# A fused attention and feed-forward kernel: each projection dealt into its attention step in two runs instead of three

## The reference

```python
xn = _layernorm(x, axis=-1)                      # x: (4, 512, 512) float32
# attention: 16 heads of 32
q, k, v = (proj(Wq, bq), proj(Wk, bk), proj(Wv, bv))
scores = einsum('bhqd,bhkd->bhqk', q, k) / sqrt(32) + alibi_bias     # causal mask
ctx = einsum('bhqk,bhkd->bhqd', softmax(scores), v)
attn = ctx @ Wo + bo
# feed-forward 512 -> 2048 -> 512, its weights rebuilt from spline control points
ffn = einsum('bsi,hi->bsh', silu(gate) * up, down_w)
return x + attn + ffn
```

## Time and profile before

| | |
|---|---|
| median of 3 runs | 837.47 us (837.46 to 837.83) |
| the profiled execution | 838.84 us |
| its span, first to last instruction | 837.0 us |
| mean granted clock of TensorE | 0.922 of full |
| busy: PE, weight loads, DVE, ACT, POOL | 711.5, 563.2, 507.2, 439.3, 332.3 us |

### The profile page before, as it was taken

One profiled execution on the slowest core, in us unless ns is written; L12 is line 12 of the kernel. 1 busy time (PEld: TensorE's weight loads), 2 busy tenths in 40 slices (PEclk: granted clock), 3 DMA queues, 4 the chain that ended last, 5 costly groups with the idle time before them and its releaser, 6 DMA issues. The chain is left out here.

```text
span 837.0 us, 14001 instructions
## 1 busy us (share of the span) xinstructions
PE 711.5 (85%) x4884; PEld 563.2 (67%) x4884; DVE 507.2 (61%) x1289; ACT 439.3 (52%) x961; POOL 332.3 (40%) x191
## 2 busy tenths in 40 slices
PE   5678779889789888898898676677978999999997
PEld 4556557667677776676676565455766888888886
DVE  6286687798979888967888688556432222222212
ACT  4266576687657766756877672334332333233321
POOL 2343453444534545534544450112214325425434
PEclk9878789899979999898999799679898999999999
DMA  7982654553584346465437945756616646433201
GB/s 254 188 219 37 111 74 155 76 76 65 114 182 101 48 76 114 93 173 77 67 68 210 252 143 170 245 153 187 208 51 196 224 118 202 153 108 105 101 1 50
DMA packets 53023, 109.78 MB, mean 131 GB/s; under 512 B 6361, under 2 KB 6617, under 8 KB 51417
## 3 DMA queue, kind: packets, MB, share of 16 engines
q1 hardware_dynamic: 51368, 106.46, 51.2%
q10 hardware_dynamic: 1584, 2.43, 1.2%
HBM read 59.32 MB, written 25.17 MB: 101 GB/s over the span
## 5 line engine op out<-in xcount | busy, mean ns | idle before, releaser
L1132 POOL TENSOR_TENSOR work<-work 128x1280 f16<-128x1280 f32 x64 | 168.4, 2632 | 235.2 <-DVE work L816 234.9
L1029 ACT ACTIVATE work<-work,neg_max 128x128 f32<-128x128 f32 (+3 forms) x256 | 142.3, 564 | 106.7 <-DVE neg_max L808 105.9
L1581 POOL TENSOR_TENSOR in_lo<-inner,in_hi 128x512 fp32r<-128x512 f32 x64 | 85.3, 1335 | 221.8 <-ACT in_hi L1497 221.8
L808 DVE CUSTOM_DVE_ANT_0 work<-bank,dist 128x128 f32<-128x128 f32 (+3 forms) x256 | 115.3, 487 | 89.0 <-PE bank L600 70.7
L1544 DVE TENSOR_TENSOR inner<-bank,silu 128x512 f32<-128x512 f32 x64 | 44.1, 689 | 136.0 <-ACT silu L1491 125.1
L1038 ACT COPY work<-bank 128x768 f16<-128x768 f16 (+1 forms) x128 | 110.0, 909 | 30.7 <-PE bank L614 29.5
L600 PE MATMUL bank<-k_stack,q_stack 96*128 96x256 f32 (+2 forms) x256 | 81.4, 396 | 45.2 <-issue 25.5
L1497 ACT CAST in_hi<-inner 128x512 fp32r<-128x512 f32 x64 | 39.7, 621 | 151.2 <-PE bank L1441 144.3
L614 PE MATMUL bank<-ident,work 128*128 128x128 f16 x1280 | 109.5, 230 | 10.2 <-DVE work L823 8.0
L614 PEld LDWEIGHTS bank<-ident,work 128*128 128x128 f16 x1280 | 78.4, 104 | 50.8 <-issue 35.2
L1439 PE MATMUL bank<-w_room,in_hi 128*128 128x512 f32 x256 | 102.7, 401 | 0.5 <-POOL in_lo L1581 0.5
(11 more groups left out here) (100 smaller groups left out, 1411.8 us busy)
## 6 DMA issues: line engine op xcount, KB each, us to landing
q_stack<-parts SPq DMA_DIRECT2D x48, 256.0 KB, 5.6
k_stack<-parts SPq DMA_DIRECT2D x48, 256.0 KB, 5.7
z<-xt_scratch SPq DMA_DIRECT2D x128, 88.0 KB
x_in<-x SPq DMA_DIRECT2D x32, 256.0 KB, 5.5
xt_scratch<-xt_room SPq DMA_DIRECT2D x8, 1024.0 KB, 6.8
xt_room<-xt_scratch SPq DMA_DIRECT2D x6, 1024.0 KB, 11.0
factor<-c_basis SPq DMA_DIRECT2D x5, 1024.0 KB, 7.9
taps<-windows SPq DMA_DIRECT2D x5, 1024.0 KB, 9.8
```

The lines of the kernel that those rows point to most:

```text
L808: dve.tensor_tensor_reduce(probs[:, s % 2, OFF[i]:OFF[i] + n], score_bank[i % 2][:, 0:n], dist[:, S - n:S], -slope(s), 3.4e38, ALU.add, AL ...
L1029: e = act.activation(tile, tile, ACT.Exp, bias=neg_max[:, s % 2, i:i + 1], scale=-1.0, accum_out=row_sum[:, s % 4, i:i + 1])
L1132: pool.tensor_tensor(probs16[:, s % 2, 1, :], probs[:, s % 2, :], probs16[:, s % 2, 0, :], ALU.subtract).then_inc(lo_ready, 1)
L1581: pool.tensor_tensor(in_lo[k % 2][:, :], inner[:, k % 2, :], in_hi[:, k % 2, :].bitcast(F32), ALU.subtract).then_inc(il_ready, 1)
```

## The change

The third and fourth contraction tile of a unit now stand together, behind `turn_probs` 1 and ahead of `weigh_values` 2. Tile 2 moves from ahead of `turn_probs` 1 to behind it; tile 3 moves from behind `weigh_values` 3 to ahead of `weigh_values` 2. Step 2 keeps its tile 2 alone. No matmul is added or left out, and no other engine's order changes.

```diff
                 if turned:
                     turn_probs(*turned, 0)
-                for key in early:
-                    unit(b, s, key, (2,))
                 if turned:
                     turn_probs(*turned, 1)
+                for key in early:
+                    unit(b, s, key, (2, 3) if s != 2 else (2,))
                 for i in range(2, QT):
                     if weighed:
                         weigh_values(*weighed, i)
-                for key in early if s != 2 else []:
-                    unit(b, s, key, (3,))
                 for i in range(2, QT):
                     if turned:
                         turn_probs(*turned, i)
```

## The result

The changed kernel takes 845.39 us (median of four runs, 844.38 to 848.22) against 837.47 us (837.05 to 837.83): a ratio of 1.010 with a 95% interval of 1.0074 to 1.0126, 7.9 us slower. The forecast was 846.1 in 841.0 to 851.5. Timed again on another chip, beside 23 runs of the kernel before with a median of 837.59, it took 845.30: 1.0097 (1.008 to 1.0114). The profiled execution after is one of 844.38 us with a span of 842.6.

What follows compares the result with a forecast made beforehand. TensorE is busiest, but VectorE's chain behind the reciprocal sets the pace; 0.9 + 2.2 + 2.9 + 2.0 + 0.9 + 0.1 = 9.0 us, 8.1 at the milder end, taken as 8.6: 837.47 becomes 846.1 us, range 841 to 851.5.

Steps and rivals of the forecast that it cites:

- `av_full` 0.67 later: Steps with a three-run unit: tile 3 ahead of `weigh_values` 2 and 3 delays VectorE's reciprocal by 0.67 us.
- the longer waits for score tiles: Steps 2 and 6: TensorE waits longer for VectorE's score tiles, starting 0.3 and 0.5 us later.
- run starts win: Rival: VectorE reaches the reciprocal late anyway, so nothing moves later and saved run starts give 833 to 836; chance 0.05.
- Run starts: 43 units in three runs save 0.11 us each, 4.7 us at most, only where TensorE alone sets the end.
- Steps 4 to 7, 2.2 us: Delay passes through v split, score tiles and GpSimd to the stack DMAs: 0.5 us, 0.67 in batch 0.
- Steps 8 and 9, 2.9 us: L839 misses its place ahead of GpSimd's L1127, x transposes 1.0 us later, three times; 2.0 if it gets in.
- Step 11, 2.0 us: First `x_low` and the whole v unit come 0.67 us later behind the moved reciprocal, three times.
- Steps 0 to 3 and 12 to 15, 0.9 us each: 0.3 us of the delay is left over and passes to later scores or the k stack, three times each.
- The last period, 0.1 us: Steps 8 to 11 of batch 3, without layer norm: 0.1 us slower.
- The clock: Rival: slow restarts behind nine stack waits, 3.0 us each; more of them, above 849, chance 0.13; fewer, no loss left, 0.06.
- Absorbed by stacks (842.5): Rival: starts of steps 0 and 8 hang on DMA traffic, 3.6 us of terms go, 5.0 left; chance 0.16.
- The feed-forward stage: Stays as it is; a length change of more than 3 us would show the forecast wrong.

Runs made afterwards that it cites:

- the third experiment: Against the kernel before, only tile 3 moved ahead of `weigh_values` 2, still three runs: 848.51 us, 1.0124.
- the second: Against the kernel before, tiles 2 and 3 in one run, but both behind `weigh_values` 3: 835.63 us, 0.9973.
- The two pauses: Kernel before plus idle VectorE reductions ahead of `normalize` in step 9 of batches 0 to 2: short one 838.99 us, long one 835.68.
- three parts: Change's order against kernel before, only in steps 8, 9, 11: 1.0043; only in 4 to 7: 0.9992; only in 0 to 2 and 12 to 15: 1.0025.
- the last experiment: Against the kernel before, tiles 2 and 3 behind `weigh_values` 3, and in steps 9 and 10 both `norm_apply` between L832 and L839: 828.75 us, 0.9899.

## Why the prediction was right, point by point

**Sign, size and mechanism were right:** 7.9 us measured, 8.1 the second time, 8.6 forecast.

- *`av_full` 0.67 later, and nothing to hide it.* VectorE waits for L634 in 39 steps, 26.5 us (35 and 20 forecast). Steps 2 and 6, where the forecast saw the longer waits for score tiles, go from 6.19 to 6.69 us and from 5.92 to 6.52 in batch 2. The order alone, without the longer run, costs more than the change does. The rival by which VectorE comes late anyway ("run starts win") is refuted.
- *Run starts.* "4.7 us at most, and only where TensorE alone sets the end": TensorE's busy time fell by 4.1. About 2.3 came through as time, by the third experiment against the change; the second has as much against before, with the earlier `av_full` in it. The forecast had taken them off within its terms and not named a sum.
- *Steps 4 to 7, 2.2 us.* In the traces 0.68 + 0.54 + 0.48 + 0.55 = 2.25 (batch 0 with some clock in it). Alone, they gave no measurable time.
- *Steps 8 and 9, 2.9 us.* Right where it was put: step 9 is 1.06, 0.87 and 1.07 us longer, at full clock in both kernels, and L837 misses its slot by 0.1. The two pauses show both sides of this slot. The forecast was wrong on one detail: it expected the x transposes of step 10 to be about 1 us late as well, but step 10 has no unit, and its length stays at 8.71 and 8.72 us in batches 0 and 1. In batch 2 it goes from 8.34 to 8.72, and that is the clock: the transposes start 6.97 us behind the step's first scores before and 6.99 after, but they run at a clock of 1.00 before and 0.55 after, and from their start to the next scores it is 1.37 and 1.73 us.
- *Step 11, 2.0 us.* From the last group of transposes to the v unit it was 1.02 us in batch 1 and is 1.81, 0.79 more; 0.11 of it is the earlier start of the transposes. The step's length hides this in the clock: 10.67 us at 0.84 before, 10.62 at 0.91 after in batch 2. In the trace of the second timing, with the step of batch 2 at 0.85, it takes 11.34, 0.67 more than before. Steps 8, 9 and 11 alone cost 3.6 us where 4.9 stood in the sum.
- *Steps 0 to 3 and 12 to 15, 0.9 us each.* The latter 0.20, 0.28 and 0.31 in the traces, 0.79. The former can be compared only where the clock is alike: steps 1 to 3 of batch 2 are 21.82 us long against 21.38, 0.44 more where 0.3 was forecast.
- *The last period, 0.1 us.* Undersized: its stretch is 2.03 longer, 1.50 of it clock in step 8, the other 0.5 us is the delay, which steps 10 and 11 pass on there too.
- *The clock.* As the cause it is refuted for most of the loss: steps 4 to 7 of batches 1 to 3 and the three steps 9 run at full clock in both kernels (1.00) and are 1.57 and 3.00 us longer, 4.6 together. What it did to the rest is open. Twice the share missing from full clock, times the span, is the time at 1.2 GHz: 123.0 us in the profile after (0.927, 842.6 us) and 130.6 in the one before (0.922, 837.0). In the first step behind a stack 3.2 us of it cost 1.5 (6.98 us at a clock of 0.77 against 5.49, below), by which the 7.6 less would be worth 3.5 us. But whole runs don't follow this rate. The four runs of the change average 124.9 us at 1.2 GHz and the five later ones 131.6, and their medians are alike. Tile 2 alone moved has 131.7 against 126.1, and no difference in time.
- *Absorbed by stacks (842.5).* Refuted by the trace: a stack start behind a longer stretch of four steps comes later by the same amount. What speaks for it is only that the change in steps 4 to 7 alone gave no measurable time.
- *The feed-forward stage.* The forecast had it unchanged. From the first scores of attention's last step to the end it is 343.9 us before and 343.7 after.

**What stays open.** The parts don't add up to the whole: 3.6 + 1.8 = 5.4 us (or 3.6 - 0.7 + 2.1 = 5.0 in three parts, all by the ratios) against 8.1. The intervals allow some of it: 1.2 us each way for the first, 1.5 for the second and 1.4 for the whole, which together make about 2.4 of the 2.7 that are missing. The first steps behind the stacks, which differ by 1.5 or 3 us from one execution to the next with the clock, are a place where parts could interact; no run isolates that.

## What to carry to other kernels

Merging short runs saves their starts, here 0.1 us each, but before joining two runs ask what stands between them and who waits for it: the piece that raises a semaphore for another engine goes first, the filler behind it (the same double run cost 7.9 us ahead of `weigh_values`; behind it the kernel is 2.5 us faster). An engine at 85% can be without a gap and still not be the one that sets the pace; look at what the second engine does within 0.1 us of each handover. And where two engines compete for memory, put the instruction that is held behind the one that the critical engine waits for.

## What was not expected of the hardware

- **The place between two GpSimd instructions is won or lost by some tenths of a microsecond.** VectorE's instruction with two SBUF inputs, 0.29 us when free, was served between two GpSimd instructions when it asked 0.21 us ahead of the end of the first, and held for the whole second one when it asked 0.25 behind it (0.10 in the profile after). `norm_apply`, with one SBUF input of 512 fp32 columns, is held in the same way: 2.35 us for two in the last experiment. The reciprocal ran while GpSimd was busy and wasn't held.
- **The clock of a restart isn't told by how long TensorE idled.** Timeline of PE after, the scores that start step 8 of batches 0 and 1:

```profile
95.81 0.48 PE L600 MATMUL bank<-k_stack,q_stack 96*128 96x256 f32 x2 [2.05 <-issue]
...
213.80 0.77 PE L600 MATMUL bank<-k_stack,q_stack 96*128 96x256 f32 x2 [2.12 <-issue]
```

The windows over the two steps, fields as above:

```profile
95.81:101.30 5.49, 5.49 (x57) 4.53 (x57) 3.65 (x13) 2.64 (x9) 2.63 (x1) 1.00 0.29 107
...
213.80:220.78 6.98, 6.98 (x56) 5.71 (x57) 3.67 (x13) 2.63 (x9) 2.63 (x1) 0.77 0.51 166
```

After 2.05 us of idle time TensorE starts at 2.4 GHz and the step takes 5.49 us, after 2.12 at 1.2 GHz and it takes 6.98. In the kernel before, 2.17 us gave the full clock again (5.57 us), and 2.82 gave 8.50 us; in the last experiment 2.91 us gave the full clock (5.52 us). One execution differs from the next by this: a median of three runs that agree within 0.4 us, as those of before did, says less than it seems, since 23 runs lie 6 us apart.
